# Four graph layers on one core: messages packed to 384 columns, a carried row added by VectorE, pairs in ascending order

## The reference, cut to what matters

```python
f   = linear(x)                       # [node, 64 + 3*32]
w   = act(edge_scalars @ fc1) @ fc2   # [edge, 192]: four weights per channel
# message of an edge: 96 scalars and 96 vectors of 3, 4*96 = 384 numbers
msg = concat(w0*f_s[src]*e0, w3*dot(f_v[src], e1), (w1*f_s[src])*e1, (w2*e0)*f_v[src])
agg = segment_sum(msg, dst)           # over the edges that end in one node
x   = layernorm(x + gate(self_term(x), linear2(agg)))
```

## Time and profile before

| | us |
|---|---|
| median of 3 runs | 4727.86 (4722.86 to 4741.2) |
| span of the profiled execution | 3876.7 |
| TensorE busy in it | 3478.5 (90%) |
| VectorE busy | 2719.2 (70%) |
| GpSimd busy | 2408.3 (62%) |
| ScalarE busy | 2215.8 (57%) |

### The profile page before, as it was taken

How to read it: one execution, slowest core, us unless ns; L and a number is a source line. 1 busy time by engine, 2 the same in 40 slices (tenths; PEclk the granted TensorE clock), 3 DMA queues, 4 the chain that set the end, 5 groups by cost and what they waited for, 6 DMA issues and landing times.

```text
span 3876.7 us, 103835 instructions
## 1 busy us (share of the span) xinstructions
PE 3478.5 (90%) x26652; PEld 3216.9 (83%) x26652; DVE 2719.2 (70%) x10601; ACT 2215.8 (57%) x6014; POOL 2408.3 (62%) x2869
## 2 busy tenths in 40 slices
PE   2899997666599999999979999999989999998887
PEld 1799997565599999877779999877779999997776
DVE  3577775888766666588866666588866666657887
ACT  0244443666544444477755555477756666658888
POOL 1477776888667777566657777500026666657776
PEclk9899998889799999999989999999989999999999
DMA  9622223777522222398832222288842222226776
GB/s 360 248 64 62 61 54 101 255 256 252 191 60 59 57 56 51 107 302 291 291 98 63 62 60 56 57 295 296 298 138 55 54 53 50 47 68 231 260 260 226
DMA packets 424013, 572.03 MB, mean 148 GB/s; under 512 B 218794, under 2 KB 242344, under 8 KB 419590
## 3 DMA queue, kind: packets, MB, share of 16 engines
q1 hardware_dynamic: 295142, 322.06, 27.6%
q0 software_dynamic: 81680, 114.98, 10.9%
q10 hardware_dynamic: 47088, 133.80, 8.7%
HBM read 356.01 MB, written 233.79 MB: 152 GB/s over the span
## 4 chain that ended last, share of the span: by engine, by line
PE 68%; DVE 13%; issue 9%; DMA 4%; ACT 2%; POOL 2%; DVEq 1%; ACTq 0%; POOLq 0%; SPq 0%
PE bank L776 18%; PE bank L809 13%; PE bank L819 5%; PE bank L766 4%; PE bank L885 4%; DVE stats L1387 3%; PE bank L832 3%; PE bank L829 3%; PE bank L783 3%; PE bank L824 3%; PE bank L888 3%; PE bank L801 3%; DVE arena L1380 2%; PE bank L858 2%; DVE mv L1398 2%
## 5 line engine op out<-in xcount | busy, mean ns | idle before, releaser
L569 POOL DMA_INDIRECT aggregates<-arena,meta x784 | 794.0, 1013 | 459.6 <-issue 253.1
L776 PE MATMUL bank<-same_all,msg 128*98 (+1 forms) x6272 | 757.5, 275 | 0.0
L556 POOL DMA_INDIRECT xg<-x_after,meta x588 | 582.2, 990 | 250.6 <-issue 245.8
L1052 ACT ACTIVATE arena<-arena,shift,rstd 128x160 f32<-128x160 f32 x1600 | 697.3, 508 | 64.5 <-DVE shift L1318 62.4
L776 PEld LDWEIGHTS bank<-same_all,msg 128*98 128x98 f32 x6272 | 714.9, 167 | 0.0
L966 ACT ACTIVATE w<-bank 1x162 f32<-1x162 f32 (+1 forms) x784 | 257.0, 328 | 739.9 <-PE bank L809 737.6
L809 PE MATMUL bank<-w,arena 98*128 98x32 f32 (+1 forms) x4704 | 627.4, 270 | 0.0
L809 PEld LDWEIGHTS bank<-w,arena 98*128 98x128 f32 x4704 | 589.3, 192 | 0.0
L1387 DVE BATCH_NORM_STATS2 stats<-arena 128x6 f32<-128x160 f32 x1600 | 453.0, 313 | 42.3 <-DVE arena L1380 8.8
L1271 DVE TENSOR_TENSOR arena<-bank,yv 128x192 f32<-128x192 f32 x294 | 105.1, 357 | 473.8 <-PE bank L829 291.9
L1026 ACT ACTIVATE nT<-bank 128x640 f32<-128x640 f32 x400 | 279.5, 699 | 252.2 <-PE bank L888 181.1
(11 more groups left out here) (156 smaller groups left out, 7167.5 us busy)
## 6 DMA issues: line engine op xcount, KB each, us to landing
arena<-aggregates SPq DMA_DIRECT2D x400, 324.0 KB, 3.9
x_after<-arena ACTq DMA_DIRECT2D x300, 320.0 KB, 4.1
arena<-x_after SPq DMA_DIRECT2D x300, 320.0 KB, 3.6
aggregates<-arena ACTq DMA_DIRECT2D x25, 1296.0 KB, 14.0
arena<-nodes SPq DMA_DIRECT2D x100, 320.0 KB, 3.9
out<-arena SPq DMA_DIRECT2D x100, 320.0 KB, 2.2
same_all<-sorted_dst SPq DMA_DIRECT2D x7, 1792.0 KB, 10.8
aggregates<-arena,meta POOLq DMA_INDIRECT x784, 2.3
```

Of the source, the lines that this page charges most:

```text
L556: gp.indirect_dma_start(xg[:, k % XGR, 4 + t * F:4 + (t + 1) * F], None, xtab[l], at).then_inc(gathered[k], 16)
L569: gp.indirect_dma_start(agg, at, tot[:, kk % TRING, t, 0:AW], None, bounds_check=NP - 1, oob_is_err=False).then_inc(spread[kk], 16)
L776: last = nc.tensor.matmul(bank[5 + t][0:MR, c * P:(c + 1) * P], msg[:, k2, t, c, :], same_all[:, bass.ds(here[t], P)], start=True, stop=True)
L1052: last = nc.scalar.activation(row, row, ACT.Identity, bias=shift[:, kk, t:t + 1], scale=rstd[:, kk, t:t + 1])
```

## The change

The messages become exactly 384 columns per tile, and 128 of them are the weights of one product: three products instead of four for the sums of a tile, to an output of 128 partitions by 3 x 128 columns. The second map uses three accumulating products over the same three blocks; its weights are laid out to match. Flag and constant leave the messages. The total that goes over from one tile to the next is kept in `carry` (384 numbers, 128 x 3) by VectorE, which also adds it into column 0 of each tile's sums (`mend`, two small instructions per tile); ScalarE copies the other 127 columns of both tiles. Pairs run in ascending order, and a tile's last edge holds what goes on. In TensorE's order both second maps move: tile 0 to after `w1`, tile 1 to after fc2. `w1` waits for `f_free` (raised by L1292) instead of `msg_ready`. The counts of layer 1 come from a reduction of `same_all`, mended by a few operations on one partition at the end of the layer's node stage.

```diff
-        msg = sb("msg", [P, 2, 2, 4, MR])
+        msg = sb("msg", [P, 2, 2, 4, MF])
+        carry = sb("carry", [P, 4, 3])
@@ TensorE, edge_products
-                        for t in (1, 0):
+                        for t in range(2):
                             wait(pe, summed_out[t], edge_count(l, q - 3))
+                            wait(pe, mended[t], edge_count(l, q - 3))
-                            for c in range(4):
-                                last = nc.tensor.matmul(bank[5 + t][0:MR, c * P:(c + 1) * P], msg[:, k2, t, c, :],
+                            sent = msg[:, k2, t].rearrange("p h f -> p (h f)")
+                            for c in range(3):
+                                last = nc.tensor.matmul(bank[5 + t][:, c * P:(c + 1) * P], sent[:, c * P:(c + 1) * P],
                                                         same_all[:, bass.ds(here[t], P)], start=True, stop=True)
...
                     def second_map(t):
                         pe.wait_ge(summed_out[t], edge_count(l, q - 2))
+                        pe.wait_ge(mended[t], edge_count(l, q - 2))
+                        if G == 1:
+                            wait(pe, tot_out[t], edge_count(l, q - 3))
+                        elif t == 0:
+                            wait(pe, tot_out[1], edge_count(l, q - 3))
+                        else:
+                            pe.wait_ge(tot_out[0], edge_count(l, q - 2))
...
+                        mm(part_of(0, first), aggT[:, t, 0, :], rows_of(0, first), start=True, stop=False)
+                        mm(part_of(first, first + 2 * V), aggT[:, t, 2, :], rows_of(first + 2 * V, first + 4 * V), start=False, stop=False)
+                        mm(part_of(first - V, first + V), aggT[:, t, 1, :], rows_of(first, first + 2 * V), start=False, stop=True)\
+                            .then_inc(tot_ready[t], 1)
@@ ScalarE, edge_copies
-                        nc.scalar.activation(aggT[:, 1, :], bank[6][0:MR, :], ACT.Copy).then_inc(summed_out[1], 1)
+                        for t in range(2):
+                            act.wait_ge(summed[t], edge_count(l, q - 2))
+                            wait(act, tot_ready[t], edge_count(l, q - 3))
+                            sums = bank[5 + t][:, 0:MC].rearrange("p (h e) -> p h e", h=3)
+                            nc.scalar.activation(aggT[:, t, :, 1:P], sums[:, :, 1:P], ACT.Copy).then_inc(summed_out[t], 1)
...
-                        nc.scalar.activation(w2[l][0:1, 1 - t, :], tb[t][0:1, 0:aw[l]], ACT.Copy).then_inc(carried[1 - t], 1)
@@ VectorE, edge_vectors
-                        nc.vector.tensor_copy(aggT[:, 0, :], bank[5][0:MR, :]).then_inc(summed_out[0], 1)
+                    if l == 1 and within(q, 0, NPAIR):
+                        nc.vector.tensor_reduce(dst_count[:, bass.ds(pair, 1), :].rearrange("p o t -> p (o t)"),
+                                                cols.rearrange("p (t e) -> p t e", t=2), AX.X, ALU.add).then_inc(counted, 1)
+                    def mend(t):
+                        kk, tt = back(k, turn, 1)
+                        dve.wait_ge(summed_out[t], edge_count(l, q - 1))
+                        wait(dve, tot_ready[t], edge_count(l, q - 2))
+                        wait(dve, carried, 2 * (q + l * NPAIR) - (2 - t))
+                        sums = bank[5 + t][:, 0:MC].rearrange("p (h e) -> p h e", h=3)
+                        at = 2 * (kk % 2) + t
+                        stt(out=carry[:, (at + 1) % 4, :], in0=carry[:, at, :], scalar=meta[:, kk, 24 + t:25 + t], in1=sums[:, :, P - 1],
+                            op0=ALU.mult, op1=ALU.add).then_inc(carried, 1)
+                        stt(out=aggT[:, t, :, 0], in0=carry[:, at, :], scalar=meta[:, kk, 4 + t:5 + t], in1=sums[:, :, 0],
+                            op0=ALU.mult, op1=ALU.add).then_inc(mended[t], 1)
...
-                    nc.vector.tensor_copy(msg[:, k2, :, :, 0], meta[:, k, 4:6, None].to_broadcast([P, 2, 4]))
+                    if G == 1:
+                        last.then_inc(f_free, 1)
+                    if within(q, 1, NPAIR):
+                        mend(0)
+                        mend(1)
                     dve.wait_ge(dprod_ready, edge_count(l, q))
```

More of the change, by code:

```diff
@@ L43 @@
 AW3 = 2 * F
-MW = 24
+MW = 26
+MF = 96
+MC = 4 * MF
+T1 = 2 + S + V
+W2C = T1 + 4 * V
+W2C3 = 2 * (S + V + 4 * V)
 XC = 4 + 2 * F + 4 + 2 * 30
@@ L128, in laid_out @@
         if l < 3:
-            o = W2_AT + AW * l
-            small[1:97, o + 2:o + 2 + S] = np.concatenate([w[x] for x in n['l2s']], axis=0)
-            for d in range(3):
-                c = o + 2 + S + V * d
-                small[1:97, c:c + V] = np.concatenate([w[x] for x in n['l2v']], axis=0)
+            o = W2_AT + W2C * l
+            of_s = np.concatenate([w[x] for x in n['l2s']], axis=0)
+            of_v = np.concatenate([w[x] for x in n['l2v']], axis=0)
             if n['ex']:
-                small[1:97, o:o + 1] = w[n['ex']]
-            if l == 1:
-                small[97, o + 1] = 1.0
+                small[0:MF, o:o + 1] = w[n['ex']]
+            small[0:MF, o + 2:o + 2 + S] = of_s
+            for c, row, first, last in V_BLOCKS:
+                small[row:row + last - first, o + T1 - V + V * c:o + T1 + V * c] = of_v[first:last]
     for j, x in enumerate(('L3_gnn_Ws_l2_a', 'L3_gnn_Ws_l2_c', 'L3_gnn_Wv_l2_a', 'L3_gnn_Wv_l2_c')):
@@ L221, in build @@
         aw = [AW, AW, AW, AW3]
[L222 removed]
+        w2 = [sb(f"w2_{l}", [P, W2C if l < 3 else W2C3]) for l in range(4)]
         meta = sb("meta", [P, RING, MW])
@@ L280, in build @@
         idx1 = part(4056, 256)
-        carry1 = part(4312, 256)
+        goes_on = part(4312, 2)
+        comes_in = part(4314, 2)
+        one_run = part(4316, 2)
+        later1 = part(4320, 256)
         sort_iota = arena[:, 4580:4580 + SORT_COLS]
@@ L738, in _ @@
             pe.wait_ge(l2_copied, 1)
-            for j in range(4):
-                a, b = (384, 448) if j < 2 else (448, 480)
-                at = (0, 64, 128, 160)[j]
-                last = nc.tensor.matmul(bank[7][0:MR, at:at + b - a], l2_rows[0:96, MR * j:MR * (j + 1)],
-                                        raw[0:96, o + a:o + b], start=True, stop=True)
+            for g in range(2):
+                strip, at = g * L2_STRIP, g * (W2C3 // 2)
+                nc.tensor.matmul(bank[7][:, at:at + S], l2_rows[0:MF, strip:strip + P], raw[0:MF, o + 384:o + 448],
+                                 start=True, stop=True)
+                for c, row, first, end in V_BLOCKS:
+                    v = strip + P + MF + first - row
+                    last = nc.tensor.matmul(bank[7][:, at + S + V * c:at + S + V * (c + 1)], l2_rows[0:MF, v:v + P],
+                                            raw[0:MF, o + 448:o + 480], start=True, stop=True)
             last.then_inc(l2_done, 1)
@@ L812, in edge_products @@
-                    if has_old:
-                        second_map(1)
-                    if has_new:
-                        wait(pe, msg_ready, edge_count(l, q - 1))
-                        if G == 1:
+                            part_of = lambda a, e: tb[t][:, a:e]
+                            rows_of = lambda a, e: w2[l][:, a:e]
+                            first = T1
+                        else:
+                            part_of = lambda a, e: by_group(tb[t][:, 0:AW3])[:, :, a:e]
+                            rows_of = lambda a, e: w2[l].rearrange("p (g c) -> p g c", g=2)[:, :, a:e]
+                            first = S + V
@@ L1161, in _ @@
             nc.vector.tensor_copy(by_field(meta_all[:, :, 4:6]), four(bank[3])[:, 2:4])
+            nc.vector.tensor_copy(by_field(meta_all[:, :, 24:26]), four(bank[0])[:, 0:2])
             nc.vector.tensor_copy(by_field(meta_all[:, :, 6:10]), four(bank[4]))
@@ L1220, in edge_vectors @@
                             dve.wait_ge(dst_in, 96)
-                        for t in (1, 0):
-                            tile = (NPAIR - 1 - q) * 2 + t
+                        for t in range(2):
+                            tile = q * 2 + t
                             cols = same_all[:, tile * P:(tile + 1) * P] if isinstance(q, int) else same_all[:, bass.ds(tile * P, P)]
@@ new lines, in edge_vectors @@
+                    if l == 3 and within(q, 3, NPAIR + 3):
+                        kk, tt = back(k, turn, 3)
+                        dve.wait_ge(tot_out[1], edge_count(l, q - 3))
+                        alone(dve, passed["dve"])
+                        nc.vector.tensor_tensor(tot[:, kk % TRING, :, 2:AW], tot[:, kk % TRING, :, 2:AW],
+                                                tot[:, kk % TRING, :, AW:AW + F], ALU.add).then_inc(tot_summed, 1)
+                    if l == 1 and within(q, 0, NPAIR):
+                        pair = q if isinstance(q, int) else dve.snap(q)
+                        cols = same_all[:, q * (2 * P):(q + 1) * (2 * P)] if isinstance(q, int) else same_all[:, bass.ds(q * (2 * P), 2 * P)]
```

(2 more changed lines are left out.)

184 lines of the change are left out of this document (88 added, 96 removed).

## The result

The kernel after takes 4588.07 us (median of 4 runs, 4572.92 to 4606.82), the kernel before on the same chip 4731.83 (4722.86 to 4741.2): ratio **0.9706, 95% interval 0.967 to 0.9742**, 143.8 us less. The forecast was 4611. On a second chip, where most experiments ran, it is 3774.17 against 3881.52, ratio **0.9727 (0.9711 to 0.9743)**, 107.4 us less.

The account below looks back on a forecast made before the run. TensorE was taken to set the pace before, GpSimd (5.24 us per pair) in layers 0 to 2 after. Gains 13 + 47 + 28 + 32 - 3 = 117 us gave 4728 - 117 = 4611 us, range 4555 to 4690.

Parts of the forecast that it names:

- TensorE's saving and GpSimd's floor: Edge stages: TensorE saves 0.78 us per pair in layers 0 to 2, where GpSimd's transfers then set 5.24 us per pair.
- TensorE's own work: Edge stages: TensorE's work per pair falls to 4.58 us in layers 0 and 2, 4.79 in layer 1, 5.55 in layer 3.
- the rival that the sums keep their 1.75: Segment sums on TensorE: loads of 128 weight columns set the pace, 83 us of gain remain, 4645 us; chance 0.04.
- Layers 0, 1, 2: Edge stages of these layers: GpSimd sets the pace, gains of 12.9, 47 and 28 us.
- The drain: Stage end in layers 0 to 2: last scatter ends 16 x 1.29 = 20.6 us after the gather of pair 97 starts.
- Layer 3: Edge stage of layer 3: pace 5.8 us per pair instead of 6.13, a gain of 32 us.
- the stall before the last second map: Layer 3, shared bank 7: tile 1's second map waits about 0.25 us per pair for ScalarE's two copies of tile 0.
- The mends: VectorE's four small instructions per pair: 1.0 us, bounds 0.6 and 2.7; above 1.7 layer 0 is VectorE's.
- the rival's own sentence: Mends hold the messages on VectorE, deciding over 1.9 us in layer 0, 2.6 in layers 1 and 2; 4990 us, chance 0.08.
- The chain after layer 1: Five dependent instructions on one partition after layer 1: 2 to 4 us added, taken as 3.
- The part outside the span: Median before lies 851 us above the profiled span of 3876.7; taken as unchanged by the change.
- proportional: Alternative for the 851 us outside the span: if it shrank in proportion, the gain would be 143 us.

## Why the prediction held, and where it did not

- **TensorE's saving and GpSimd's floor.** Right on the second chip. 5.24 was forecast and 5.21 measured, L787 waits for gathers, and the pace goes down with one scatter less (4.76). The product put back costs 2 to 8 us in each of these stages against 43 in layer 3.
- **TensorE's own work.** The sums cost (2103.36 - 2102.02) / 12 = 0.112 per instruction with 128 columns of weights against 0.109 with 98, 1.34 us per pair in place of 1.75: the rival that the sums keep their 1.75 falls. By the prediction's own estimate the loads of the sums were 2 x 0.656 = 1.31 us per pair before, less than the 1.75 measured, so they could not have held the sums there. (Its sum was off as well: with layer 3 at 6.24, 0.11 slower than before, 74 us remain and not 83.) TensorE's own work was put at 4.79 in layer 1, where 4.76 is measured, and at 4.58 in layers 0 and 2, where the pace of 4.76 holds a wait of 0.15 to 0.2 us for VectorE. It cost nothing here, being below 5.21.
- **Layers 0, 1, 2.** 17.1, 50.8 and 29.3 us for 12.9, 47 and 28. The drain, worked out as 16 transfers of 1.29 without waits, 20.6 us, takes 20.8 in layers 1 and 2; in layer 0 it is 22.2, with two waits for ScalarE in it. Of the 4.2 us in layer 0, 2.1 are the yardstick: that stage of before takes 589.6 us here and 587.4 in the trace that I had read, from 58.6 to its last scatter. The rest is that the gather of pair 97 did not stay where it was but came 3.7 us earlier after the start of the stage, less the 1.6 of the longer drain.
- **Layer 3.** The step that failed in size is the stall before the last second map: 0.25 forecast, 0.36 measured. Its terms were 0.3 from the last instruction of tile 0's map to ScalarE, 0.65 for the two copies and 0.1 for the signal, which is 1.05, less 0.77; measured are 0.31, 0.68 and 0.14, which is 1.13. The slow start of the waiting map, 0.07, was not in the sum. With TensorE's own work at 5.53 to 5.56, the pace is 5.99 and not 5.8, and the stage gains 16.6 us, not 32. The mechanism is the one named: with other work between the two maps the stall is gone and the stage is 42.6 us shorter.
- **The mends.** Taken at 1.0 us per pair; in the trace the four and their waits run from 3070.82 to 3071.83 in one pair of layer 3, 1.01. That they would decide from 1.7 us on in layer 0 (1.9 in the rival's own sentence) was too low: at 2.1 they are still covered. The step added busy time of VectorE (4.3 us in layer 0) that was the pace less one wait, gaps at semaphores included.
- **The chain after layer 1.** Taken at 3 us, measured 0.6 (351.5 to 352.1 us between the stages).
- **The part outside the span.** Wrong. I subtracted the gain of one chip from the time of another. The 851 us are no launch cost; in the kernel after they are edge stages that take longer on such a chip, and the gain there was 143.8 us, not 117. That is nearly the 143 that the prediction gave for "proportional", but nothing shows that a gain has to be in proportion. That 4611 lies 23 us from 4588.07 is in part luck: GpSimd's floor of 5.24 can't be what holds stages that run at 7.1 to 8.0 us per pair, so the account of layers 0 to 2 is shown for the second chip alone. The forecast is too high by 143.8 - 117 = 27, less 4 by which the median of before moved, 23. On the second chip 3881.5 - 117 = 3764.5 is 9.7 too low, mostly for layer 3.

What stays open is what makes the edge stages long on the first chip. Windows of the first profile of after:

```profile
160.00:800.00 640.00, 495.97 (x3266) 442.71 (x3265) 355.81 (x1417) 190.69 (x530) 353.49 (x356) 0.86 0.21 52
1320.00:1950.00 630.00, 486.68 (x3410) 466.79 (x3409) 300.46 (x998) 185.22 (x499) 327.61 (x329) 0.86 0.19 43
2420.00:3060.00 640.00, 477.76 (x3156) 426.73 (x3156) 288.29 (x938) 235.74 (x683) 332.93 (x335) 0.87 0.19 44
3510.00:4190.00 680.00, 544.92 (x3738) 504.91 (x3737) 366.69 (x1131) 312.39 (x870) 353.79 (x342) 0.94 0.18 41
```

Waits of ScalarE in layer 1, there, and then on the second chip, both the kernel after:

```profile
ACT arena L993 <- remote: 160.1, 62, 4.3
ACT arena L993 <- PE bank L830: 143.4, 75, 3.4
ACT arena L978 <- remote: 69.7, 36, 3.3
```

```profile
ACT arena L993 <- PE bank L830: 129.8, 135, 1.0
ACT arena L978 <- PE bank L799: 32.7, 138, 0.4
```

No engine is busy for more than some 80% of these windows. ScalarE waits up to 4.3 us in layer 1 for signals that the trace can't put down to an instruction, and with the idle time the granted clock is down at 0.86 to 0.94 as a mean. The shared semaphore is not it, for the kernel before has none and takes 4731.83 there. The kernel before was not profiled on such a chip, so it is not shown where its 851 us lie, nor why the change gains 143.8 us there and 107.4 on the other.

## What to carry to other kernels

Work out the floor of every engine that waits for nothing in its own timeline, not from its busy share: GpSimd at 62% busy was 0.15 to 0.37 us per pair away from being the bound of layers 0 to 2, and a cut of 0.78 on TensorE was worth only that much, and shorter drains. When two products share a bank, price the work that lies between them before you move either. And compare time and span of one and the same execution; a median that stands 22% above a span is a question, not a constant.

## What the runs showed of the hardware

- A loop whose code is unchanged can lose 59 us in a stage of 411 because instructions were added ahead of it: 5 packets of 8 KB are fetched per turn, VectorE stands still for some 4 us at each jump back, and with 64 empty instructions ahead of it, on another chip, both the packets and the 59 us are gone. This agrees with the Trainium skill (Runtime: NRT & Kernel Launch, section Instruction fetch mechanics), by which an engine holds only two blocks of its instructions, and a jump to one that it no longer holds waits for a fetch.
- An indirect transfer costs GpSimd 0.94 to 1.05 us in over nine of ten cases, 1.00 as the median, and 0.30 between two, for a gather as for a scatter here, and on both kinds of chip alike.
- A float32 product with 128 columns of weights and 128 streamed costs TensorE 0.112 us per instruction against 0.109 with 98 columns of weights. With 128 columns of weights and 32 to 98 streamed it is hardly cheaper: 0.103 as the mean of the 8 instructions of a second map before, 0.112 of the 6 after.
- The same program can take 3774 us on one chip and 4588 on another; the node stages agree within 2% (412.8, 357.4 and 344.2 us against 411.2, 352.1 and 342.9), the edge stages don't (749.6 against 512.8 in layer 2), and the ratio of the two kernels is the same within its interval.
